# The selective scan of an eight-layer program: C's rows by DMA from memory, and four of sixteen C products on GpSimd

## What is computed

```python
xdbl = jnp.einsum('bld,de->ble', xc, W_xproj)       # xc: after convolution and silu
dt_r, Bm, Cm = xdbl[..., :8], xdbl[..., 8:24], xdbl[..., 24:40]
dt = softplus(dt_r @ W_dt + b_dt)
A = -jnp.exp(A_log)
def step(h, inp):                                   # over the 512 tokens
    dt_t, B_t, C_t, u_t = inp
    h = h * jnp.exp(dt_t[:, :, None] * A) + dt_t[:, :, None] * B_t[:, None, :] * u_t[:, :, None]
    return h, jnp.einsum('bdn,bn->bd', h, C_t)
y = (scan(step) + xc * D_param) * silu(z)
out = x + y @ W_out
```

## Time and profile before

| | us |
|---|---|
| median of 3 runs | 2709.16 (2704.49 to 2710.79) |
| the profiled execution | 2704.73, span 2703.0, clock 0.959 |

### The profile page before, as it was taken

How to read it: one execution, slowest core, us unless ns; L and a number is a source line. 1 busy time by engine, 2 the same in 40 slices (tenths; PEclk the granted TensorE clock), 3 DMA queues, 4 the chain that set the end, 5 groups by cost and what they waited for, 6 DMA issues and landing times. The chain is left out here.

```text
span 2703.0 us, 42649 instructions
## 1 busy us (share of the span) xinstructions
PE 2478.8 (92%) x13288; PEld 1584.1 (59%) x13316; DVE 1738.7 (64%) x4099; ACT 1451.4 (54%) x2938; POOL 1617.9 (60%) x1421
## 2 busy tenths in 40 slices
PE   7995999997778999987499899999999999999999
PEld 4664998685763434433499544444444455777777
DVE  4436554764437999998666699999999981111112
ACT  2340443433458887774244577777777764343333
POOL 4652776531568999996255477677776761997000
PEclk9997999897899999999699899999999999999999
DMA  9010443401122222221701198888888882000001
GB/s 301 25 36 22 145 143 115 132 1 32 36 73 68 81 77 80 77 79 50 238 25 27 32 200 194 192 192 192 189 192 194 192 196 61 9 16 9 9 8 32
DMA packets 144678, 268.33 MB, mean 99 GB/s; under 512 B 28491, under 2 KB 68310, under 8 KB 144454
## 3 DMA queue, kind: packets, MB, share of 16 engines
q1 hardware_dynamic: 132342, 245.45, 35.4%
q0 software_dynamic: 9088, 18.63, 2.5%
q10 hardware_dynamic: 3024, 1.52, 0.2%
HBM read 96.74 MB, written 24.32 MB: 45 GB/s over the span
## 5 line engine op out<-in xcount | busy, mean ns | idle before, releaser
L1775 POOL TENSOR_TENSOR l3a_p_all<-l3a_p_all,l3a_rden 128x1024 f32<-128x1024 f32 x256 | 483.8, 1894 | 202.9 <-DVE l3a_rden L1850 202.8
L1908 ACT ACTIVATE l3a_p_all<-l3a_p_all,l3a_low 128x512 f32<-128x512 f32 x512 | 364.3, 713 | 130.9 <-DVE l3a_low L1845 129.6
L1845 DVE CUSTOM_DVE_ANT_0 l3a_p_all<-bank,relative_bias 128x512 f32<-128x512 f32 x512 | 331.8, 686 | 55.1 <-PE bank L1974 31.4
L1858 DVE STREAM_TRANSPOSE l3a_blocks<-l3a_p_all 128x1024 f32<-128x1024 f32 x256 | 313.9, 1235 | 1.8 <-issue 1.8
L2770 POOL TENSOR_TENSOR l2a_dBu<-l2a_du,l2a_bs 128x1024 f32<-128x1024 f32 x128 | 298.5, 2352 | 17.6 <-DVE l2a_h L3015 15.4
L3015 DVE TENSOR_TENSOR_SCAN l2a_h<-bank,l2a_dBu 128x1024 f32<-128x1024 f32 x128 | 290.8, 2280 | 13.8 <-POOL l2a_dBu L2770 7.8
L1832 DVE SCALAR_TENSOR_TENSOR x<-bank,l3a_blocks,x 128x128 f32<-128x128 f32 x256 | 71.9, 344 | 336.5 <-PE bank L2049 336.3
L1923 ACT ACTIVATE relative_bias<-bank,l3a_b 128x512 f32<-128x512 f32 x224 | 153.0, 688 | 214.4 <-PE bank L2039 210.8
L1974 PE MATMUL bank<-l3a_kT,l3a_qT 64*128 64x512 f32 x1024 | 244.4, 604 | 4.0 <-DVE l3a_low L1845 3.5
L2000 PE MATMUL bank<-l3a_pT,l3a_v 128*64 128x512 f32 x1024 | 233.8, 598 | 0.1
L2039 PE MATMUL bank<-relative_xnT_all,relative_w_qk 128*128 128x512 f32 x512 | 230.4, 594 | 0.0
(11 more groups left out here) (529 smaller groups left out, 4995.8 us busy)
## 6 DMA issues: line engine op xcount, KB each, us to landing
l3a_pT<-l3a_blocks SPq DMA_DIRECT2D x1024, 128.0 KB, 2.4
l2a_bs<-l2a_b_rows SPq DMA_DIRECT2D x128, 256.0 KB, 3.1
l0fe_wv<-expert_weights SPq DMA_DIRECT2D x71, 256.0 KB
by_place<-by_distance SPq DMA_DIRECT2D x16, 512.0 KB, 12.5
relative_bias<-by_place SPq DMA_DIRECT2D x16, 448.0 KB, 11.1
expert_weights<-in_L_ffn_in_dram SPq DMA_DIRECT2D x1, 4096.0 KB, 29.0
l0f_answers<-l0f_y_rows SPq DMA_DIRECT2D x16, 256.0 KB, 5.2
relative_w_qk<-in_L_ffn_W_dram SPq DMA_DIRECT2D x16, 256.0 KB, 3.2
```

Source lines behind the costliest of these rows:

```text
L1775: p_ready.by(pool.tensor_tensor(a, a, bcast(rden[g % 2][:, t, :], n_after=S), ALU.mult))
L1845: bk.drain(dve.tensor_tensor_reduce(p_of(g, t)[:, h, :], ps(job)[:], bias[:, u * 2 + h, b0:b0 + S], 1.0, 3.0e38, ALU.add, ALU.min, low[:, ...
L1858: ins = dve.transpose(out, p_of(g, t).rearrange("p h (k b j) -> p (h k) b j", b=Q, j=32))
L1908: ins = act.activation(a, a, ACT.Exp, bias=low[:, t, h:h + 1], scale=-1.0, accum_out=den[:, t, h:h + 1])
```

## The change

C takes the way of B: ScalarE stores all 32 rows (B and C) of a batch row in `bc_rows`, and SP fetches row C of step k into one of NK = 6 tiles `cs`, in its queue two steps (BEHIND) after B's. Both weighings read `cs`, in SBUF. `spread`, `pick`, `c_bank`, `c_rows`, `bc` and the splitting are gone. GpSimd weighs states 0, 3, 6 and 9, VectorE the other twelve; their adding up is at n = 6, 10, 13 and 15. `add_step` and `weigh_step` come at n = 11 and 12. The bank that `c_bank` had is named `spare_bank` and is written only by the products that keep TensorE running ahead of the loop.

```diff
-        self.w_tap, self.pick = sb("w_tap", [P, TAPS, DI]), sb("pick", [P, N, P], BF16)
+        self.w_tap = sb("w_tap", [P, TAPS, DI])
...
         for k in range(TAPS):
...
-    NA, NB, ND, NH, NC = 2, 4, 3, 5, 3
+    NA, NB, ND, NH, NC, NK, BEHIND = 2, 4, 3, 5, 3, 6, 2
...
-        c_bank, y_bank = chip.psum[4], chip.psum[5:7]
-        b_rows = nc.dram_tensor("l2a_b_rows", (B, N, S), F32, kind="Internal").ap()
+        spare_bank, y_bank = chip.psum[4], chip.psum[5:7]
+        bc_rows = nc.dram_tensor("l2a_bc_rows", (B, 2 * N, S), F32, kind="Internal").ap()
...
         M = B * N
-        SHARED, LATER, ADDED_AT = (0, 3, 6), 4, {0: 6, 3: 12, 6: 13}
+        SHARED, LATER, ADDED_AT = (0, 3, 6, 9), 4, {0: 6, 3: 10, 6: 13, 9: 15}
...
-                for m in range(M):
-                    q, n = divmod(m, N)
-                    if n == 0:
-                        sp.wait_ge(b_stored, 16 * (q + 1))
-                    if m >= NB:
-                        sp.wait_ge(dBu_ready, m - NB + 1)
-                    sp.dma_start(bs[m % NB][:], b_rows[q, n, :].partition_broadcast(P)).then_inc(b_loaded[m % NB], 16)
+                for m in range(M + BEHIND):
+                    if m < M:
+                        q, n = divmod(m, N)
+                        if n == 0:
+                            sp.wait_ge(bc_stored, 16 * (q + 1))
+                        if m >= NB:
+                            sp.wait_ge(dBu_ready, m - NB + 1)
+                        sp.dma_start(bs[m % NB][:], bc_rows[q, n, :].partition_broadcast(P)).then_inc(b_loaded[m % NB], 16)
+                    k = m - BEHIND
+                    if k >= 0:
+                        if k - NK in dve_no:
+                            sp.wait_ge(hc_ready, dve_no[k - NK] + 1)
+                        if k - NK in pool_no:
+                            sp.wait_ge(hp_ready, pool_no[k - NK] + 1)
+                        sp.dma_start(cs[k % NK][:], bc_rows[k // N, N + k % N, :].partition_broadcast(P)).then_inc(c_loaded[k % NK], 16)
 
             @block.gpsimd
             def _(pool):
                 def weigh(m):
                     k = pool_no[m]
-                    pool.wait_ge(c_copied, k + 1)
+                    pool.wait_ge(c_loaded[m % NK], 16 * (m // NK + 1))
                     pool.wait_ge(h_ready, m + 1)
                     if k >= 2:
                         pool.wait_ge(hc_summed, add_no[of_pool[k - 2]])
-                    pool.tensor_tensor(hp[k % 2][:], h[m % NH][:], bcast(c_rows[k % 2][:], n_before=CH), ALU.mult).then_inc(hp_ready, 1)
-
-                def split_left(q):
-                    pool.wait_ge(hi_ready, q + 1)
-                    pool.wait_ge(raw_ready, q + 1)
-                    pool.tensor_tensor(left[:], raw[:], bc[q % 2][0:2 * N, :], ALU.subtract).then_inc(left_ready, 1)
-
-                def split_last(q):
-                    pool.wait_ge(mid_ready, q + 1)
-                    pool.tensor_tensor(left[:], left[:], mid[:], ALU.subtract).then_inc(left2_ready, 1)
+                    pool.tensor_tensor(hp[k % 2][:], h[m % NH][:], bcast(cs[m % NK][:], n_before=CH), ALU.mult).then_inc(hp_ready, 1)
...
-                        if n == (5 if q else 7):
-                            split_left(q + 1)
-                        if n == 10:
-                            split_last(q + 1)
+                        if n == 11:
+                            add_step(q + 1, slice(0, CH))
                         if n == 12:
-                            add_step(q + 1, slice(0, CH))
-                        if n == 13:
                             weigh_step(q + 1, slice(0, CH))
...
-                def take_c(m):
-                    k = pool_no[m]
-                    act.wait_ge(C_ready, m + 1)
-                    if k >= 2:
-                        act.wait_ge(hp_ready, k - 1)
-                    act.copy(c_rows[k % 2][:], c_bank[:]).then_inc(c_copied, 1)
...
-                    if q:
-                        act.wait_ge(left2_ready, q)
...
-                    act.dma_start(b_rows[q], raw[0:N, :]).then_inc(b_stored, 16)
...
-                def split_first(q):
-                    if q >= 2:
-                        act.wait_ge(C_ready, (q - 1) * N)
-                    act.copy(bc[q % 2][0:2 * N, :], raw[:]).then_inc(hi_ready, 1)
-
-                def split_mid(q):
-                    act.wait_ge(left_ready, q + 1)
-                    act.copy(mid[:], left[:]).then_inc(mid_ready, 1)
-
-                def split_done(q):
-                    act.wait_ge(left2_ready, q + 1)
-                    act.copy(bc[q % 2][PART:PART + 2 * N, :], mid[:])
-                    act.copy(bc[q % 2][2 * PART:2 * PART + 2 * N, :], left[:]).then_inc(bc_ready, 1)
+                    act.wait_ge(raw_ready, q + 1)
+                    act.dma_start(bc_rows[q], raw[:]).then_inc(bc_stored, 16)
...
-                act.wait_ge(cleared, 1)
-                split_first(0)
...
-                split_mid(0)
...
-                split_done(0)
...
-                    if m in pool_no:
-                        take_c(m)
...
                 def weigh(m):
                     k = dve_no[m]
-                    dve.wait_ge(C_ready, m + 1)
+                    dve.wait_ge(c_loaded[m % NK], 16 * (m // NK + 1))
                     dve.wait_ge(h_ready, m + 1)
                     if k >= NC:
                         dve.wait_ge(hc_summed, add_no[of_dve[k - NC]])
-                    dve.tensor_tensor(hc[k % NC][:], h[m % NH][:], bcast(c_bank[:], n_before=CH), ALU.mult).then_inc(hc_ready, 1)
+                    dve.tensor_tensor(hc[k % NC][:], h[m % NH][:], bcast(cs[m % NK][:], n_before=CH), ALU.mult).then_inc(hc_ready, 1)
...
-                def spread(m):
-                    if m >= M:
-                        return
-                    q, n = divmod(m, N)
-                    if n == 0:
-                        pe.wait_ge(bc_ready, q + 1)
-                    if m - 1 in dve_no:
-                        pe.wait_ge(hc_ready, dve_no[m - 1] + 1)
-                    if m - 1 in pool_no:
-                        pe.wait_ge(c_copied, pool_no[m - 1] + 1)
-                    pe.matmul(c_bank[:], pick[:, n, :], bc[q % 2][:], start=True, stop=True).then_inc(C_ready, 1)
...
                     for j in range(CH):
-                        ins = pe.matmul(y_bank[j][:], chip.ident[:], weighed[:, j, :], start=False, stop=(m % N == N - 1))
+                        ins = pe.matmul(y_bank[j][:], chip.ident[:], weighed[:, j, :], start=False, stop=(m == adds[(m // N + 1) * N - 1]))
...
-                keep_running(5, c_bank)
-                spread(0)
+                keep_running(5, spare_bank)
```

More of the change, by code:

```diff
@@ L2614, in prepare @@
             pool.tensor_tensor(self.w_tap[:, k, :], self.w_in[:, 0:DI], self.tap_rows[:, k, :], ALU.mult)
-        pool.tensor_copy(self.pick[:], bcast(self.part_of[:, N:2 * N], n_after=P))
         for j in range(CH):
@@ L2631, in selective_scan @@
     nc = chip.nc
-    PART = 32
-    NA, NB, ND, NH, NC = 2, 4, 3, 5, 3
+    NA, NB, ND, NH, NC, NK, BEHIND = 2, 4, 3, 5, 3, 6, 2
     PARTS = ((0, TPS), (TPS, 2 * TPS), (2 * TPS, NT))
@@ L2642, in selective_scan @@
         ln_w, ln_b, conv_b, b_dt = held.ln_w, held.ln_b, held.conv_b, held.b_dt
-        pick, d_diag, a_neg = held.pick, held.d_diag, held.a_neg
+        d_diag, a_neg = held.d_diag, held.a_neg
         both_eps, warm = sb("both_eps", [P, 1]), sb("warm", [P, 1])
@@ L2652, in selective_scan @@
         dt, du = two("dt", [P, CH, S]), two("du", [P, CH, S])
-        raw, dtr, left, mid = sb("raw", [2 * N, S]), sb("dtr", [R, S]), sb("left", [2 * N, S]), sb("mid", [2 * N, S], BF16)
-        bc = two("bc", [P, S], BF16)
-        bs = [sb(f"bs{k}", [P, S]) for k in range(NB)]
+        raw, dtr = sb("raw", [2 * N, S]), sb("dtr", [R, S])
+        bs, cs = ([sb(f"{n}{k}", [P, S]) for k in range(c)] for n, c in (("bs", NB), ("cs", NK)))
         dBu, h, hc = ([sb(f"{n}{k}", [P, CH, S]) for k in range(c)] for n, c in (("dBu", ND), ("h", NH), ("hc", NC)))
-        hp, c_rows = two("hp", [P, CH, S]), two("c_rows", [P, S])
-        hp_ready, c_copied = sem("hp_ready"), sem("c_copied")
+        hp, hp_ready = two("hp", [P, CH, S]), sem("hp_ready")
         dA = [chip.banks[:, CH * k:CH * (k + 1), :] for k in range(NA)]
-        c_bank, y_bank = chip.psum[4], chip.psum[5:7]
-        b_rows = nc.dram_tensor("l2a_b_rows", (B, N, S), F32, kind="Internal").ap()
+        spare_bank, y_bank = chip.psum[4], chip.psum[5:7]
+        bc_rows = nc.dram_tensor("l2a_bc_rows", (B, 2 * N, S), F32, kind="Internal").ap()
         M = B * N
-        SHARED, LATER, ADDED_AT = (0, 3, 6), 4, {0: 6, 3: 12, 6: 13}
+        SHARED, LATER, ADDED_AT = (0, 3, 6, 9), 4, {0: 6, 3: 10, 6: 13, 9: 15}
         of_pool = [m for m in range(M) if m % N in SHARED]
@@ L2684, in selective_scan @@
         mv_ready, gains_ready, rows_ready, x_normed = sem("mv_ready"), sem("gains_ready"), sem("rows_ready"), sem("x_normed")
```

(28 more changed lines are left out.)

## The result

The changed kernel takes 2779.95 us (median of 4 runs, 2779.26 to 2788.09) against 2709.97 (4 runs, 2704.49 to 2713.37) for the kernel before: ratio 1.0266, interval 1.0244 to 1.0287, slower by 70 us. The forecast was 2779.

The account below looks back on a forecast made before the run. GpSimd and VectorE in lock step were taken to bound the kernel. GpSimd's stream 494 + end 13 + idle 5 = 512 us against 441.2, +71, less 1.3 at the start: net +70, 2779 us, range 2757 to 2816.

Parts of the forecast that it names:

- The block: In the scan loop, VectorE's weighing with two SBUF inputs and GpSimd's SBUF-reading operations run one after another; chance 0.62.
- Its price: Cost of one VectorE weighing to GpSimd's stream: 1.08 us less 0.11 hidden, 0.97 us.
- Rival 2: Whole 1.20 us records of VectorE's weighings add to GpSimd's stream: 523 in place of 494, 2808 us; chance 0.12.
- The sum: From GpSimd's first dBu to VectorE's last x write: 494 + 13 + 5 = 512 us against 441.2.
- GpSimd's stream without its waits: Over the scan: 402 us of GpSimd operations, 1.0 late gains, 91 for 94 VectorE weighings, together 494.
- GpSimd's idle time in it: GpSimd's waits during the scan: 5 us taken, bounds 0 and 20, against 15.4 + 4.8 before.
- from its end to the last write of x: Scan's end after GpSimd's last dBu: 12.1 us plus 0.9 for one more pair of products, 13.
- start of the stretch: Around GpSimd's first dBu: 0.5 us from the dropped cast of raw and 0.8 from L3055, -1.3.
- (d): C's rows on SP's queue: one more 256 KB transfer per step, landing in 3.1 to 6.2 us, hidden.
- Rival 4: TensorE's clock falls to 1.2 GHz for one whole batch row, adding 27 us: 2806; chance 0.04.
- The first paragraph: Scan of the kernel before: GpSimd and VectorE work in lock step, so each us put on either shows.
- rival 1: No blocking in the loop: row falls from 54.2 to 52.5 us, -15, 2694; chance 0.07 with weaker forms.

Follow-up runs that it names:

- a_psum_const: Changed kernel with VectorE's weighing reading its second factor from a PSUM bank (not C, y wrong): ratio 1.0022 to the kernel before.
- b_sbuf_const: Kernel before with VectorE's weighing reading its second factor from a constant SBUF tile (not C, y wrong): ratio 1.0412 to the kernel before.
- d_three: Changed kernel with three GpSimd weighings (states 0, 3, 6) and thirteen on VectorE: ratio 1.0200 to the kernel before.
- e_one2: Changed kernel with one GpSimd weighing (state 0) and fifteen on VectorE: ratio 1.0127 to the kernel before.
- k_before_nd42: Kernel before with four buffers for dBu and five for B's rows, nothing else: ratio 0.9996 to the kernel before.
- n_hp3: a_psum_const with four dBu buffers, five for B, GpSimd's states added at 5, 8, 11, 14, three buffers for GpSimd's products: ratio 1.0008 to the kernel before.

## Why the prediction was right, point by point

**The block.** Right, and shown: one operand moved takes it away (a_psum_const) or brings it (b_sbuf_const). Three records ahead of the loop were enough to forecast it. The rule of the Trainium skill ("SBUF — State Buffer", "Who interferes with whom") says that VectorE with two SBUF inputs and a GpSimd instruction that reads SBUF contend, and that whoever issues first goes first. The first half is what the traces show. The second fails in b_sbuf_const if a record's start tells who came first: two later GpSimd operations went ahead in seven cases, and five in one.

**Its price.** Forecast 0.97 us per weighing. Measured on GpSimd's records: 128 x (2.794 - 2.352) + 32 x (3.107 - 2.352) + 7 x (3.187 - 2.360) = 86.6 us, over 94 weighings 0.92. By the stream from start to start, which holds the gaps of some 0.13 us between records too, it is (494 - 402 - 1) / 94 = 0.97. The same sum gives 1.00 in d_three ((486.0 - 383.5 - 1) / 102) and 0.97 in e_one2 ((461.6 - 346.5 - 1) / 118). Rival 2 (1.20) is out.

**The sum.**

| | forecast, us | measured, us |
|---|---|---|
| GpSimd's stream without its waits | 494 | 494 (1335.99 - 832.23 = 503.8, less 9.8 of waits) |
| GpSimd's idle time in it | 5 (0 to 20) | 9.8 |
| from its end to the last write of x | 13 | 16.0 |
| start of the stretch | -1.3 | -1.9 |
| net | +70 | +76.6 (519.7 - 441.2 - 1.9) |

The profiled execution went from 2704.73 to 2780.49, +75.8; the medians, 2709.97 to 2779.95, +70.0. So that the median was met to 1 us is partly luck: the profiled execution of before was at the low end of its runs and that of after wasn't. The sum's own error is some 7 us, in two terms. Idle time: the one wait of 8.0 us, for the adding up of state 3 in the last row, which stands behind VectorE's weighing of state 10; I had judged GpSimd's waits as a whole and not followed this place, and some 3 us of it are TensorE's clock, as shown above. The end: 16.0 us in place of 13. Of the 3.0 more, 1.1 come since VectorE's weighing of state 13 stands between GpSimd's last dBu (end 1335.99) and the last recurrence (start 1337.10). The products for state 9 at n = 15 put 1.7 on it, where I had 0.9. The last 1.0 is TensorE's clock again: 0.72 of full speed was granted from 1336 to 1342 us, and two groups of four products took 2.64 and 2.97 us in place of 1.88.

**C's rows by DMA, (d).** Right: 3.5 and 3.3 us to landing, DMA share 0.43, nobody waits for them.

**TensorE's clock.** Rival 4 came true in small: 0.90 and 0.91 in the rows shown, 0.97 before. In the middle rows TensorE had waits for VectorE's weighing to lose (85.5 us in the stretch), so as far as the rows show the clock cost only in the last row and the end: some 3 us of the 8.0 us wait and 1.0 of the end.

**What failed.** The first paragraph said that GpSimd and VectorE bind the kernel before and rival 1 that without a block the row falls from 54.2 to 52.5 us, 15 us in all. a_psum_const has no block and rows of 54.5, k_before_nd42 shows that GpSimd's lead wasn't the bound before, and n_hp3 that freeing GpSimd of every wait but that for h moves nothing. The step that failed is rival 1's floor for the row: the 50.8 us of GpSimd and VectorE with 1.7 of waits. I had TensorE's 51.4 busy us of 54.2 and took the smaller sums of the other two as floors that could be reached. "ScalarE and TensorE are not what the end waits for" was said of the sum and is nearly true there, but it doesn't carry over to a row without the block. What holds that row at 54 us is not shown; TensorE's order is the reading above. The failed step did not touch the forecast: with the block GpSimd's own stream, 494 us, is longer than anything else and sets the time. But had the operand been in PSUM I would have promised 15 us that are not there.

## What to carry to other kernels

Before a VectorE operand moves from PSUM to SBUF, look at what GpSimd does at that time. If the VectorE instruction then has two SBUF inputs and GpSimd reads SBUF, add their times (here 0.92 to 1.00 us for each of 1.20) instead of taking the larger. The recurrence, with one input in SBUF, kept its 2.28 us. A lengthened duration of an instruction whose shape hasn't changed is the sign, as no idle time shows. With three engines each busy over 93% of a row, as before the change, freeing GpSimd alone (k_before_nd42) was worth nothing here; know the others' order first.

## What was not expected of the hardware

A VectorE instruction that waits for GpSimd can be passed by more than one GpSimd instruction: 7.01 us for a 1.20 us operation in b_sbuf_const, and once 13.8. In the changed kernel none waited for more than one. What tells them apart is open.
